# Null-key attention: scores from float32r parts with both heads on the array's rows, and transposes ahead of the next scores

## The reference, cut to what matters

```python
q = einsum('bnd,df->bnf', layernorm(x), Wq)          # 4 x 256 x 1024
k, v = split(einsum('bmc,cf->bmf', ctx, Wkv))
k = concatenate((null_k, k)); v = concatenate((null_v, v))   # 257 keys
sim = einsum('bhid,bhjd->bhij', q * 64 ** -0.5, k)
attn = softmax(sim)
out = einsum('bhij,bhjd->bhid', attn, v)             # then Wout and a layer norm, added to x
```

## Time and profile before

| what | us |
|---|---|
| median of 3 runs (lowest, highest) | 1356.1 (1355.16, 1358.35) |
| profiled execution, its own time | 1356.21 |
| its span | 1354.4 |
| TensorE busy in the span | 1155.1 (85%) |
| VectorE, ScalarE, GpSimd busy | 808.1, 681.6, 525.6 |
| first scores of the stage to its last values product | 1071.36 to 1260.23 |

### The profile page before, as it was taken

The page is one execution under the profiler, slowest core; times in us unless marked ns, Lnnn a source line. Parts: engine busy times, 40 slices in busy tenths (PEclk is TensorE's granted clock), DMA queues, the critical chain, the costliest instruction groups (busy, mean ns, idle before and its releaser), DMA issues.

```text
span 1354.4 us, 18006 instructions
## 1 busy us (share of the span) xinstructions
PE 1155.1 (85%) x6098; PEld 807.3 (60%) x6098; DVE 808.1 (60%) x1922; ACT 681.6 (50%) x1623; POOL 525.6 (39%) x670
## 2 busy tenths in 40 slices
PE   4468699999828999887989999968999799999767
PEld 2236477777612444655667777745777567676655
DVE  8744588888768772477667776664111344444454
ACT  2223377666511555365757877752433365655121
POOL 8200467777750000043647666672000243344110
PEclk7577699999965997889889999986999899999979
DMA  4311000000012230120000000314000100000000
GB/s 158 110 48 54 0 1 1 0 1 1 0 52 66 99 98 2 36 90 0 1 1 1 0 1 1 125 52 172 1 0 1 64 0 1 1 1 1 1 1 16
DMA packets 24540, 42.73 MB, mean 32 GB/s; under 512 B 3424, under 2 KB 22144, under 8 KB 23168
## 3 DMA queue, kind: packets, MB, share of 16 engines
q1 hardware_dynamic: 24448, 41.58, 8.7%
HBM read 36.95 MB, written 4.46 MB: 31 GB/s over the span
## 4 chain that ended last, share of the span: by engine, by line
PE 67%; DVE 16%; ACT 8%; POOL 3%; issue 3%; DMA 1%; SPq 1%; DVEq 0%; ACTq 0%; POOLq 0%
PE psum L1410 7%; PE psum L1031 5%; PE psum L1021 5%; PE psum L770 4%; PE psum L1991 4%; PE psum L780 4%; ACT region_d L1476 3%; PE psum L336 3%; PE psum L298 3%; PE psum L309 3%; PE psum L2029 2%; PE psum L1397 2%; PE psum L1979 2%; PE psum L1974 2%; PE psum L2005 2%
## 5 line engine op out<-in xcount | busy, mean ns | idle before, releaser
L1410 PE MATMUL psum<-gated_parts 128*128 128x512 f32 x768 | 198.5, 413 | 16.7 <-DVE region_d L1581 15.8
L1410 PEld LDWEIGHTS psum<-gated_parts 128*128 128x128 f32 x768 | 142.6, 193 | 68.7 <-DVE region_d L1581 33.3
L1650 POOL TENSOR_TENSOR region_d<-region_d 128x256 f32<-128x256 f32 x128 | 102.5, 801 | 119.2 <-DVE region_d L1581 117.8
L132 POOL TENSOR_TENSOR rstd<-var_eps,minus_half 128x4 f32<-128x4 f32 x16 | 16.3, 1024 | 324.1 <-DVE var_eps L92 322.0
L1106 ACT ACTIVATE rounds_work<-psum,region_c 128x512 f32<-128x512 f32 x128 | 87.0, 689 | 60.9 <-PE psum L1021 60.9
L1269 POOL TENSOR_TENSOR parts<-rounds_work,parts 128x512 fp32r<-128x512 f32 x64 | 108.9, 1722 | 0.0
L1172 DVE TENSOR_TENSOR parts<-rounds_work,parts 128x512 fp32r<-128x512 f32 x64 | 84.8, 1362 | 27.4 <-POOL parts L1266 27.4
L2102 DVE TENSOR_REDUCE work_behind<-psum 128x2 f32<-128x514 f32 x64 | 44.4, 694 | 91.3 <-PE psum L1991 90.7
L1031 PE MATMUL psum<-parts,split 128*128 128x512 f32 x384 | 98.1, 405 | 0.0
L1476 ACT ACTIVATE region_d<-psum,gated_work 128x128 f32<-128x128 f32 x256 | 75.1, 439 | 45.0 <-issue 26.2
L1581 DVE SCALAR_TENSOR_TENSOR region_d<-psum,ctx,region_d 128x128 f32<-128x128 f32 x256 | 71.7, 343 | 43.1 <-ACT region_d L1476 39.6
(11 more groups left out here) (374 smaller groups left out, 2411.7 us busy)
## 6 DMA issues: line engine op xcount, KB each, us to landing
region_a<-in_l1v SPq DMA_DIRECT2D x1, 4096.0 KB, 12.9
work_behind<-in_l1o SPq DMA_DIRECT2D x1, 4096.0 KB, 12.1
region_a<-in_l2f SPq DMA_DIRECT2D x1, 4096.0 KB, 13.3
work_behind<-in_l3f_small SPq DMA_DIRECT2D x1, 4096.0 KB, 19.7
region_a<-in_l3f SPq DMA_DIRECT2D x1, 2080.0 KB, 8.1
region_c<-in_l0f SPq DMA_DIRECT2D x1, 2076.0 KB, 12.2
region_c<-in_l3x SPq DMA_DIRECT2D x1, 2048.0 KB, 7.9
front_work<-q_parts SPq DMA_DIRECT2D x24, 64.0 KB
```

The costliest lines, as they stand in the source:

```text
L1410: ins = pe.matmul(bank[2 * (n % 2) + c], src[a][:, t * P:(t + 1) * P], weights[b][:, piece(c)], start=m == 0, stop=m == len(PASSES) - 1)
L1650: pool.tensor_tensor(tile[:, 0:2, :], tile[:, 0:2, :], tile[:, 2:4, :], ALU.add).then_inc(k.pool_chain, 1)
```

## The change

Three things are changed in this stage. The scores are computed from two float32r parts of query and key (a high part, and the rest), as high x high + high x low + low x high, and the two heads of a pair use the upper and lower 64 rows of the array at the same time (`tile_position` j*64), with 258 columns (the null key is stored twice). The query is stored once, scaled; `half` goes. VectorE gets an instruction for each query and key chunk that forms the low part from PSUM, and the projections and scores wait for it (`proj_low`). And TensorE's list is reordered: both turns of a sequence come first, then the scores of both heads of the next sequence, then projections and values product as before. VectorE's other work, ScalarE's and GpSimd's keep their order. The parts lie in a buffer of their own (`open_null`), and two of the output tiles in the context's buffer.

```diff
-    q = [[k.carve(F32, T) for _ in range(2)] for _ in range(2)]
-    kT = [k.carve(F32, B, NK) for _ in range(2)]
+    parts = k.null_parts
+    q_part = [[parts[:, (2 * i + a) * T:(2 * i + a + 1) * T] for a in range(2)] for i in range(2)]
+    NK2 = NK + 1
+    PASSES = ((0, 0), (0, 1), (1, 0))
...
+    oT += [free_ctx[:, i * T:(i + 1) * T] for i in range(2)]
...
             if n >= 2:
                 pe.wait_ge(proj_sb, n - 1)
+                before, chunk = divmod(n - 2, len(CHUNKS))
+                if chunk < 4:
+                    pe.wait_ge(*proj_low.at(4 * before + chunk + 1))
...
-        def scores(g):
-            p, b, j = g // ITEMS, g % ITEMS // 2, g % 2
-            if j == 0 and b % 2 == 0:
+        def scores(p, b):
+            g = ITEMS * p + 2 * b
+            if b % 2 == 0:
                 pe.wait_ge(proj_sb, len(CHUNKS) * p + b + 2)
+                pe.wait_ge(*proj_low.at(4 * p + b + 2))
             if g >= 2:
-                pe.wait_ge(exp_ready, g - 1)
+                pe.wait_ge(exp_ready, g)
             for t in range(TPB):
                 tt = b * TPB + t
-                ins = pe.matmul(bank[2 * (g % 2) + t][:, 0:NK], q[p % 2][j][:, tt * P:(tt + 1) * P],
-                                kT[p % 2][:, b, :], start=True, stop=True)
-            ins.then_inc(score_psum, 1)
+                for n, (c, d) in enumerate(PASSES):
+                    for j in range(2):
+                        rows = slice(j * DH, (j + 1) * DH)
+                        ins = pe.matmul(bank[2 * j + t][:, 0:NK2], q_part[p % 2][c][rows, tt * P:(tt + 1) * P],
+                                        k_part[p % 2][d][rows, b, :], start=n == 0, stop=n == len(PASSES) - 1,
+                                        tile_position=(j * DH, 0))
+                        if t == TPB - 1 and n == len(PASSES) - 1:
+                            ins.then_inc(score_psum, 1)
...
-        pe.wait_ge(null_ready, 1)
-        scores(0)
-        scores(1)
+        pe.wait_ge(null_ready, 4)
+        scores(0, 0)
         for p in range(PAIRS):
             for b in range(B):
                 g = ITEMS * p + 2 * b
-                for i in range(2):
-                    if g + i + 2 < ITEMS * PAIRS:
-                        scores(g + i + 2)
-                    turn(g + i)
+                turn(g)
+                turn(g + 1)
+                if g + 2 < ITEMS * PAIRS:
+                    scores(*divmod(B * p + b + 1, B))
                 if p + 1 < PAIRS:
                     for c in MADE_IN[b]:
                         project(p + 1, c)
...
             if what == "q":
-                for j in range(2):
-                    ins = act.activation(q[p % 2][j][:, h * HALF:(h + 1) * HALF], src, ACT.Copy, scale=W("half")[:, j:j + 1])
+                ins = act.activation(q_part[p % 2][0][:, h * HALF:(h + 1) * HALF], src, ACT.Copy, scale=scale)
...
+        def low_projections(p, c):
+            n, h = len(CHUNKS) * p + c, c // 2
+            src = bank[6 + n % 2]
+            dve.wait_ge(proj_sb, n + 1)
+            if CHUNKS[c] == "q":
+                ins = dve.scalar_tensor_tensor(out=q_part[p % 2][1][:, cols], in0=src, scalar=scale,
+                                               in1=q_part[p % 2][0][:, cols].bitcast(F32), op0=ALU.mult, op1=ALU.subtract)
+            else:
+                ins = dve.tensor_tensor(k_part[p % 2][1][:, 2 * h:2 * h + 2, 0:S], src.rearrange("p (b n) -> p b n", b=2),
+                                        high.bitcast(F32), ALU.subtract)
+            ins.then_inc(proj_low.semaphore, 1)
...
+        for c in range(4):
+            low_projections(0, c)
         maxima(0)
...
             if more:
                 reciprocals(g + 3)
+            p, b = divmod(g // 2, B)
+            if p + 1 < PAIRS and b < 2:
+                for c in MADE_IN[b]:
+                    low_projections(p + 1, c)
...
         for i in range(2):
-            ins = pool.tensor_copy(kT[i][:, :, S:NK], W("nk").unsqueeze(1).broadcast_to([P, B, 1]))
-        ins.then_inc(null_ready, 1)
+            pool.tensor_copy(k_part[i][0][:, :, S:NK2], null).then_inc(null_ready, 1)
+        pool.wait_ge(null_ready, 2)
+        for i in range(2):
+            pool.tensor_tensor(k_part[i][1][:, :, S:NK2], null, k_part[i][0][:, :, S:NK2].bitcast(F32), ALU.subtract)\
+                .then_inc(null_ready, 1)
```

More of the change, by code:

```diff
@@ L1908, in null_key_attention @@
     MADE_IN = ((0, 1), (2, 3), (4,), (5,))
-    k.carve_from(REGION_B)
-    q = [[k.carve(F32, T) for _ in range(2)] for _ in range(2)]
-    kT = [k.carve(F32, B, NK) for _ in range(2)]
+    parts = k.null_parts
+    q_part = [[parts[:, (2 * i + a) * T:(2 * i + a + 1) * T] for a in range(2)] for i in range(2)]
+    NK2 = NK + 1
+    k_part = [[parts[:, 4 * T + (2 * i + a) * B * NK2:4 * T + (2 * i + a + 1) * B * NK2].rearrange("p (b n) -> p b n", b=B)
+               for a in range(2)] for i in range(2)]
+    PASSES = ((0, 0), (0, 1), (1, 0))
+    scale = float(DH) ** -0.5
+    k.carve_from(0)
     V = [k.carve(F32, NT, P) for _ in range(2)]
@@ L1924, in null_key_attention @@
     oT = [free_a[:, p * T:(p + 1) * T] for p in range(in_a)]
-    oT += [k.carve(F32, T) for _ in range(PAIRS - in_a)]
+    free_ctx = k.ctx_sb[:, :, :].rearrange("p t c -> p (t c)")
+    oT += [free_ctx[:, i * T:(i + 1) * T] for i in range(2)]
+    oT += [k.carve(F32, T) for _ in range(PAIRS - in_a - 2)]
     EN = k.carve(F32, NT, 2 * PAIRS)
@@ L1939, in null_key_attention @@
     proj_sb = sem("proj_sb")
+    proj_low = k.count("packed_rest", 4 * PAIRS)
     score_psum = sem("score_psum")
@@ L2065, in projections @@
             if what == "q":
-                for j in range(2):
-                    ins = act.activation(q[p % 2][j][:, h * HALF:(h + 1) * HALF], src, ACT.Copy, scale=W("half")[:, j:j + 1])
+                ins = act.activation(q_part[p % 2][0][:, h * HALF:(h + 1) * HALF], src, ACT.Copy, scale=scale)
             elif what == "k":
-                ins = act.activation(kT[p % 2][:, 2 * h:2 * h + 2, 0:S], src.rearrange("p (b n) -> p b n", b=2), ACT.Copy)
+                ins = act.activation(k_part[p % 2][0][:, 2 * h:2 * h + 2, 0:S], src.rearrange("p (b n) -> p b n", b=2), ACT.Copy)
             else:
@@ L2115, in copy_turned @@
             dve.tensor_copy(PT[g % 4].rearrange("p a n -> p (a n)"), bank[4 + g % 2]).then_inc(pt_sb, 1)
+        def low_projections(p, c):
[3 more added lines that the diff above has]
+            if CHUNKS[c] == "q":
+                cols = slice(h * HALF, (h + 1) * HALF)
+                ins = dve.scalar_tensor_tensor(out=q_part[p % 2][1][:, cols], in0=src, scalar=scale,
+                                               in1=q_part[p % 2][0][:, cols].bitcast(F32), op0=ALU.mult, op1=ALU.subtract)
+            else:
+                high = k_part[p % 2][0][:, 2 * h:2 * h + 2, 0:S]
+                ins = dve.tensor_tensor(k_part[p % 2][1][:, 2 * h:2 * h + 2, 0:S], src.rearrange("p (b n) -> p b n", b=2),
[3 more added lines that the diff above has]
+            low_projections(0, c)
         maxima(0)
@@ L2153, in gpsimd @@
         pool.wait_ge(k.weights[name], 32)
+        null = W("nk").unsqueeze(1).broadcast_to([P, B, 2])
         for i in range(2):
-            ins = pool.tensor_copy(kT[i][:, :, S:NK], W("nk").unsqueeze(1).broadcast_to([P, B, 1]))
-        ins.then_inc(null_ready, 1)
+            pool.tensor_copy(k_part[i][0][:, :, S:NK2], null).then_inc(null_ready, 1)
[3 more added lines that the diff above has]
+                .then_inc(null_ready, 1)
         pool.wait_ge(k.norm.ready, NT * (use + 1))
@@ L2549, in build @@
             stages.append(dense_experts(k, "l2f", 5, 8, k.weight_views("l2f", L2F, "l2f_small", L2F_SMALL), routing=False))
+        k.open_null()
         if last_stage >= 7:
@@ L2708, in close_gated, with open_null @@
         self.region["B"] = self.work[:, 0:REGION_B]
+    def open_null(self):
+        self.work_extent.close()
+        self.region["B"] = self.work_extent.enter_context(self.nc.sbuf_tensor("region_b_last", [P, REGION_B], F32))
+        self.null_parts = self.work_extent.enter_context(self.nc.sbuf_tensor("null_parts", [P, NULL_PARTS], F32R))
+        self.work = self.work_extent.enter_context(self.nc.sbuf_tensor("null_work", [P, WORK - REGION_B - NULL_PARTS], F32))
     def release_work(self, kept):
@@ L2752 @@
 SPLIT = 4096
+NULL_PARTS = 4 * 1024 + 4 * 4 * 258
 GATED_PARTS = 10 * 1024
@@ L2765 @@
 L3X = (("k", 2, 8 * P), ("v", 2, 8 * P))
-L3X_SMALL = (("q", 8 * P), ("o", 8, P), ("nv", 8, 16), ("nk", 1), ("half", 2), ("ln_scale", P), ("ln_bias", P))
+L3X_SMALL = (("q", 8 * P), ("o", 8, P), ("nv", 8, 16), ("nk", 1), ("ln_scale", P), ("ln_bias", P))
 L3F = (("down", 32, P), ("router", 32), ("falling", 32))
@@ L2901, in pack @@
     nv = np.zeros((2, 64, 8, 16), np.float32)
-    half = np.zeros((2, 64, 2), np.float32)
     for j in range(2):
-        half[j, :, j] = 64.0 ** -0.5
         for p in range(8):
@@ L2907, in pack @@
```

(2 more changed lines are left out.)

## The result

The changed kernel takes 1379.4 us (median of four, 1375.6 to 1387.8) against 1355.6 for the kernel before on the same chip, a ratio of 1.0185 with a 95% interval of 1.0146 to 1.0223. It is slower, as forecast, by 23.8 us where 15.9 were forecast.

What follows compares the result with a forecast made beforehand. TensorE's work was taken to set the pace of 28 items. The new loop, 5.92 + 14 x 6.56 + 16 x 6.19 = 196.8 us against 181.3, with tail -0.3 and head +0.7, gave +15.9 on 1356.2: 1372.1, range 1359 to 1400.

Steps and rivals of the forecast that it cites:

- The rounds: Periods of the stage's loop per item: 6.56 us with query and key chunks, otherwise 6.19.
- the projections' evacuations, 0.63 each: ScalarE's copies of projections after the second head's exp, ahead of emptying bank 4: 0.63 us each, 1.26 for two.
- no longer binds: TensorE's own work per item, 5.25 or 4.46 us, is below the periods of 6.56 and 6.19.
- Scores: An item's twelve float32r score matmuls: six passes of 0.13 us with heads side by side, 0.78 us.
- Rival 1: Heads don't run side by side: scores take 1.56 us, all in the loop, +24 on top, 1396 us; chance 0.25.
- Rival 2: TensorE's clock falls to 1.2 GHz: 2.7 us more in each of 16 items, +43 on top, 1415 us; chance 0.06.
- 80 and 72%: TensorE's busy share in the stage's loop, down from 100%: 5.25 of 6.56 us and 4.46 of 6.19.
- The sum: Stage's loop 196.8 us against 181.3, tail -0.3, head +0.7: +15.9 us on 1356.2, giving 1372.1.
- Head: Stage's start: VectorE's subtractions hold a projection's bank, so the fourth chunk waits; +0.7 us.
- Rivals 3 and 4: Not slower, periods down to 5.78 us, 1354.5 us, chance 0.07; and no overlap lost, 1326 us, chance 0.04.
- rival 4: No overlap was lost in the stage because TensorE's work is what counts: 1326 us; chance 0.04.
- Edits at nothing: VectorE's subtractions, GpSimd's two further null-key copies, output tiles kept elsewhere and the smaller weight block: no cost counted.

Runs made afterwards that it cites:

- e2_order_only: The kernel before, float32 scores untouched, with both turns of a sequence ahead of the next sequence's scores: 1379.7 us, ratio 1.0165.
- e1_scores_first: The changed kernel with the next sequence's scores put back ahead of this sequence's two turns: 1334.8 us, ratio 0.9837.
- e5_same_rows: The changed kernel with both heads' score matmuls on array rows 0 to 63, head 0 computed twice: 1404.1 us, ratio 1.0352.
- e6_filled_gaps: The changed kernel with unread float32 matmuls in TensorE's idle time behind the first scores and in the last pair: 1369.7 us, ratio 1.0099.

## Why the prediction was right, and where it was off

**The mechanism held.** In-order issue turned each item's softmax into a loop with the turns and the scores. e2_order_only shows it with none of the new arithmetic, and e1_scores_first takes it away with all of it.

**The rounds.** Forecast 6.19 us for an item with a values chunk, measured 1139.26 - 1132.98 = 6.28 in the profile after. Its steps, counted from the first score matmul (1132.98):

```profile
1134.00 0.69 DVE L2114 TENSOR_REDUCE null_work<-psum 128x2 f32<-128x514 f32 x1 [3.14 <-PE psum L2004]
...
1134.72 0.48 ACT L2071 ACTIVATE null_work<-psum,null_work 128x257 f32<-128x257 f32 x1 [2.89 <-DVE null_work L2114]
...
1135.80 0.16 DVE L2121 RECIPROCAL null_work<-null_work 128x2 f32<-128x2 f32 x1
...
1136.60 1.08 PE L2043 MATMUL psum<-null_work 128*64 128x256 f32 x8 [0.66 <-DVE null_work L2127]
...
1137.73 0.38 ACT L2101 ACTIVATE region_a<-psum 128x256 f32<-128x256 f32 x1 [0.30 <-PE psum L2043]
1138.26 1.07 PE L2020 MATMUL psum<-ident,null_work 128*128 128x128 f32 x8 [0.57 <-ACT region_a L2101]
```

Maximum at 1.02 (forecast 0.96), exp at 1.74 (1.69), reciprocal at 2.82 (2.79), values product at 3.62 (3.59), bank 4 emptied from 4.75 (4.72), turn at 5.28 (5.22), next scores 1.00 later (0.97).

For an item with a query and a key chunk 6.56 was forecast and 6.34 to 6.35 measured. The step that failed is "the projections' evacuations, 0.63 each": they follow each other at 0.48, in the chain above at 1143.23, 1143.71 and 1144.20. I had halved the 1.26 us of two activations that take their scale from a tile. Groups of ScalarE by line and form, kernel before (xcount, busy us, mean ns), show that these are longer than plain copies:

```profile
L2068 ACT ACTIVATE work_behind<-psum,region_d 128x512 f32<-128x512 f32 x28 | 17.7, 688 | 0.0
L2070 ACT ACTIVATE work_behind<-psum 128x512 f32<-128x512 f32 x14 | 8.4, 598 | 1.5
```

The changed kernel's copies are plain, 0.60 long, and the next one starts 0.12 before such a one ends; the 0.57 between the two of 0.69 shows the same 0.12. Two intervals of 0.48 instead of 0.63 make 0.3 us, 14 items 4 us; the scores, 0.06 later than forecast, took a part back. A second step was off in the same item: TensorE's work "no longer binds". Scores and projections were reckoned at 0.78 + 2.58 = 3.36 us, less than the 3.59 at which the values product was forecast; they take 0.91 + 2.78 = 3.69, so the product starts when they end and not with the second copy, and TensorE's own work lies in this item's loop too. That is part of why TensorE was busy 86% of the time and not 75 to 80.

**Scores.** Forecast 0.78 us, measured 0.92, the forecast's weakest row being one extrapolated from 512 columns. The passes themselves are 0.12 us apart, as forecast (0.13); 0.1 is lost once, between the first couple and the second. Because VectorE follows the group's last pass, only 0.06 of it is seen at the first maximum.

**Rival 1** (heads not side by side, 0.25) is out: e5_same_rows is that rival made real, 0.62 to 0.68 us per item in the loop (forecast 0.78) and 1404 us (1396). The Trainium skill (TensorEngine Tiling (Array Packing), Key Properties) says that tiles work independently and can load weights and multiply in parallel; the trace agrees, 0.92 against 1.60 us. The Trainium skill's price of a weight load (TensorE: Matmul & The Clock Gate, LDWEIGHTS), the columns over 1.2 GHz however few the rows, makes 1.28 us of twelve loads one behind the other, an estimate. The whole group of loads and matmuls took 0.92, so the loads of the two row tiles did not stand in one queue.

**Rival 2** (the clock) was given 0.06 as a fall through 16 items at +43 us. It came in a form that the prediction had not listed, a small one on top of the forecast: at the second item and in the last rounds. In the profiled execution the second item took 7.93 us instead of 6.34, the last two rounds 6.76 and 8.72 instead of 6.27, and the end 9.57 instead of 7.29: 1.6 + 0.5 + 2.4 + 2.3 = 6.8 us. The rival's price of an item at half clock was near, 2.7 us against 8.72 - 6.27 = 2.45. e6_filled_gaps takes the loss away. The argument against the rival held "80 and 72%", the shares of items with projections, against the 75% of the last items of before. It left out the items without projections and the long first wait, and these are where the clock fell: in the last rounds, and behind 3.29 us in which TensorE stood idle in the first item. TensorE's share just before it did, in the kernel after:

```profile
1265.00:1270.00 5.00, 2.36 (x26) 1.84 (x27) 2.68 (x6) 2.04 (x8) 1.10 (x3) 1.00 0.00 0
1270.00:1275.00 5.00, 3.73 (x26) 2.68 (x22) 0.69 (x3) 0.38 (x1) 1.30 (x3) 0.66 0.01 3
```

**The sum.** In the stage, first scores to last values product, 196.8 + 7.2 = 204.0 us were forecast. e6_filled_gaps, at full clock, took 203.1; the change at its own clock 209.75. That 204.0 and 203.1 agree so well is in part because two errors cancel: 14 rounds were 0.21 shorter than forecast, 16 rounds 0.09 longer. So 1372 was the time of the loop without the clock's share, which e6_filled_gaps has (1369.7), and 1379.4 is that with it. The range took it in because its upper end had been set at 1400 for rival 1, which did not come; of the 23.8 us measured the sum had named 15.9. Head: +0.9 against +0.7.

**Rivals 3 and 4** are out: no period lies below 5.83 in the middle of the stage, and the saving on TensorE (rival 4's 1326) is what e1_scores_first gets with the order undone, 1334.8. It falls short of 1326 by terms that can be read: TensorE's rounds fell by 0.86 (6.39 to 5.53) and 0.87 (5.61 to 4.74), not 0.96; the last rounds, bound by the softmax, only by 0.26 (4.90 to 4.64); the head is longer; and the clock fell at the end.

**Edits at nothing** stayed that: VectorE's subtractions, GpSimd's null-key copies and the output tiles kept elsewhere appear nowhere in the chain of waits above, and e1_scores_first, which holds them all, is 22 us faster than before.

## What to carry to other kernels

Where an engine issues in order, ask of every moved step which results must now be ready before the instruction behind it, and follow that chain round until it returns: if it closes on itself, its length is the period, and work saved outside it is worth nothing. Reckon the engine's own work between two waits as one of the routes: here it tied with the longest route through the softmax. Software pipelining (working on the next item while this one still waits for other engines) is a property of the order: the scores of the next item belong ahead of the transposes of this one, and with that order the cheaper scores are worth 22 us, in the other some 8 at full clock. When a change leaves TensorE idle in pieces of 2 to 3 us, price the work of those rounds at 1.2 GHz too, as an addition to the forecast and not only as a rival.

## What the runs showed of the hardware that was not expected

- Matmuls on two row tiles ran side by side in both orders of issue: 0.92 us for twelve with the heads alternating and with three of one head at a time; on one row tile 1.60.
- The rows of ScalarE's activations are 0.12 us longer than the interval at which they follow each other: 0.60 long and 0.48 apart as plain copies of 128x512, float32r or float32 output alike in length (0.60 and 0.598), 0.688 long and 0.57 apart with a scale from a tile.
- TensorE's granted clock fell to 0.50 in rounds where it stood idle 2.64 us at a stretch, stayed at 1.00 where the fill left 0.73 and in e2_order_only with stretches of 1.78 (and one of 2.44 in the first item), and in e1_scores_first held 1.00 for two rounds with stretches of 1.62 before it fell to 0.83. What decides is not told apart here.
- The same code before the stage differed by 8.9 us between two profiled executions. 5.7 of them arose in one piece of work, 21.87 us long before (101.66 to 123.53) and 27.56 after (104.76 to 132.32), where the same matmul groups ran at a lower granted clock (0.77 and 0.58 from 100 to 125 us); the waits for transfers from 60 to 140 us were 9.1 us in both. One profiled execution is no place to read a few us of the total from; the stage's own length is.
